# Cross attention of a fused Perceiver block: decay scans in another order, key transposes in 32-column pieces

## The reference, cut to what matters

```python
# first stage: 32 heads of 8, context of 2 x 2048 rows
q = (layernorm(x) @ Wq.T)            # b n (h d)
kv = concat([ctx @ Wk.T, ctx @ Wv.T], -1).reshape(b, m, 32, 8, 2)
k, v = kv[..., 0], kv[..., 1]
q, k = rmsnorm(q), rmsnorm(k)        # over the 8 of a head
x = x + softmax(q k^T / sqrt(8)) v   # over all 2048 context rows
...
# summary of the second block, over the same context
s_t = sigmoid(decay) * s_(t-1) + (ctx_t @ W_in.T + b_in)
summary = mean over t of (s_t @ W_out.T + b_out)
```

## Time and profile before

| | us |
|---|---|
| median of 3 runs | 450.17 |
| lowest, highest | 449.66, 450.70 |
| the profiled execution | 449.79 |
| its span, first to last instruction | 448.0 |
| busy in it: PE, DVE, ACT, POOL | 399.9, 310.7, 250.4, 221.3 |

### The profile page before, as it was taken

The page is one execution under the profiler, slowest core; times in us unless marked ns, Lnnn a source line. Parts: engine busy times, 40 slices in busy tenths (PEclk is TensorE's granted clock), DMA queues, the critical chain, the costliest instruction groups (busy, mean ns, idle before and its releaser), DMA issues.

```text
span 448.0 us, 12553 instructions
## 1 busy us (share of the span) xinstructions
PE 399.9 (89%) x5149; PEld 333.5 (74%) x5149; DVE 310.7 (69%) x697; ACT 250.4 (56%) x494; POOL 221.3 (49%) x269
## 2 busy tenths in 40 slices
PE   6769999999999999879979977789789888999997
PEld 4546666677667777678979955668679877889996
DVE  5677878887888786557798876574998967322221
ACT  2447878778887888775545514521923044544541
POOL 2267656666666773334544620510489742544440
PEclk9979999999999999999999989999899999999999
DMA  4076651543311101620000080250000052000000
GB/s 149 0 262 229 206 172 45 164 127 91 105 32 44 30 15 47 247 113 1 0 1 2 1 321 3 79 244 1 0 2 1 1 227 102 1 0 2 0 2 23
DMA packets 10537, 34.67 MB, mean 77 GB/s; under 512 B 2160, under 2 KB 7280, under 8 KB 8688
## 3 DMA queue, kind: packets, MB, share of 16 engines
q1 hardware_dynamic: 10336, 33.34, 21.4%
q10 hardware_dynamic: 144, 0.52, 0.5%
HBM read 33.60 MB, written 0.26 MB: 76 GB/s over the span
## 4 chain that ended last, share of the span: by engine, by line
PE 52%; DVE 27%; POOL 10%; ACT 5%; issue 4%; DMA 1%; SPq 0%; DVEq 0%; POOLq 0%; ACTq 0%
PE ps L1075 7%; PE ps L1576 7%; PE ps L1532 6%; PE ps L1061 6%; PE ps L1546 3%; PE ps L395 3%; DVE sb_big L1315 2%; PE ps L1563 2%; POOL sb_arena L984 2%; PE ps L456 2%; PE ps L381 2%; DVE sb_arena L1325 2%; PE ps L746 2%; POOL sb_mid L998 2%; DVE sb_big L1313 2%
## 5 line engine op out<-in xcount | busy, mean ns | idle before, releaser
L1499 ACT ACTIVATE sb_arena<-ps 128x1024 f32<-128x1024 f32 x128 | 123.4, 1020 | 26.4 <-PE ps L1563 26.3
L1576 PE MATMUL ps<-sb_arena 128*25 128x128 f32 (+1 forms) x2048 | 69.4, 276 | 0.3 <-ACT sb_arena L1499 0.3
L1576 PEld LDWEIGHTS ps<-sb_arena 128*25 128x25 f32 (+1 forms) x2048 | 50.7, 98 | 7.7 <-ACT sb_arena L1499 0.8
L1532 PE MATMUL ps<-sb_halves 128*128 128x512 f32 x192 | 55.4, 425 | 0.9 <-DVE sb_arena L1325 0.9
L1105 POOL TENSOR_TENSOR sb_halves<-sb_big,sb_halves 128x704 fp32r<-128x704 f32 x20 | 33.7, 1687 | 38.8 <-ACT sb_halves L1099 38.8
L485 POOL TENSOR_TENSOR sb_halves<-sb_big,sb_halves 128x256 fp32r<-128x256 f32 x32 | 23.7, 760 | 44.9 <-ACT sb_halves L469 44.9
L1171 DVE SCALAR_TENSOR_TENSOR sb_arena<-ps,sb_w_q,sb_arena 128x176 f32<-128x176 f32 x40 | 15.9, 401 | 42.7 <-ACT sb_arena L1123 42.5
L1532 PEld LDWEIGHTS ps<-sb_halves 128*128 128x128 f32 x192 | 35.3, 197 | 13.5 <-issue 5.9
L1398 POOL TENSOR_TENSOR sb_big<-sb_arena 128x256 f32<-128x256 f32 x31 | 19.0, 613 | 52.3 <-DVE sb_arena L1286 52.3
L1075 PE MATMUL ps<-sb_halves 128*128 128x352 f32 x240 | 42.9, 332 | 2.0 <-POOL sb_halves L1105 2.0
L1075 PEld LDWEIGHTS ps<-sb_halves 128*128 128x128 f32 x240 | 39.1, 189 | 3.3 <-DVE sb_arena L1171 1.7
(11 more groups left out here) (223 smaller groups left out, 871.0 us busy)
## 6 DMA issues: line engine op xcount, KB each, us to landing
sb_big<-in_w_gu SPq DMA_DIRECT2D x2, 3520.0 KB, 11.8
sb_arena<-in_ctx SPq DMA_DIRECT2D x32, 128.0 KB, 2.3
sb_mid<-in_w_down SPq DMA_DIRECT2D x1, 3584.0 KB, 12.7
sb_mid<-in_w_ffn SPq DMA_DIRECT2D x3, 768.0 KB, 5.3
sb_big<-in_w_q SPq DMA_DIRECT2D x2, 1024.0 KB, 6.5
sb_big<-in_w_k SPq DMA_DIRECT2D x2, 1024.0 KB, 7.1
sb_big<-in_w_v SPq DMA_DIRECT2D x2, 1024.0 KB, 6.0
sb_mid<-in_w_o SPq DMA_DIRECT2D x2, 1024.0 KB, 6.0
```

The costliest lines, as they stand in the source:

```text
L1499: nc.scalar.activation(probs[:, n % P_SLOTS].rearrange("p a g n -> p a (g n)"), ps[:, bank:bank + 2], ACT.Exp, scale=XD ** -0.5).then_inc( ...
L1532: i = T.matmul(ps[:, 7], ctx_half[:, t % 2, c, kt], wkv_half[:, d, kt], start=(n + kt == 0), stop=(n == 2 and kt == KT - 1))
L1576: i = T.matmul(ps[32 * gg:32 * gg + m, 6, j * P:(j + 1) * P], v_sb[:, t % V_SLOTS, 4 * gg + j, head], probs[:, n % P_SLOTS, a, gg], start= ...
```

## The change

- `w_xq` is loaded through ScalarE's DMA queue, behind `w_xkv`, no longer through SyncE's; the load of ScalarE's function table stands ahead of both.
- On VectorE, `decay_rate()` goes to the front of the key work, `decay_weights(0)` behind `mean_squares_q(0)`, `decay_weights(1)` behind `mean_squares(1)`; in the loop, the scan of step t goes from the head of the step to behind `take_v(t + 2)`.
- The value copies of tile 0 go from VectorE to ScalarE, behind the squares of the first keys; `take_queries(1)` goes behind `key_rstd(0)`. The clearing of `v_sb` gets a semaphore of its own.
- On TensorE, `project(1)` goes ahead of `turn_queries(0)`, and four `keep_warm` calls (6, 4, 6 and 4 matmuls) are put into the start.
- In `turn_keys`, each transpose of 128 columns of packed keys becomes four of 32 columns, each into 32 partitions of the output.

```diff
--- before.py
+++ after.py
@@ -201,7 +201,6 @@
             sp.dma_start(x[:], io["x"].rearrange("b l d -> l b d")).then_inc(sem("x_loaded"), 16)
             sp.dma_start(id32[:], io["id32"]).then_inc(sem("x_loaded"), 16)
             sp.dma_start(ctxT[:, 0], io["ctx"][0]).then_inc(sem("ctx_loaded0"), 16)
-            sp.dma_start(w_xq, io["w_xq"]).then_inc(sem("wq_loaded"), 16)
             sp.dma_start(decay[:], io["decay"]).then_inc(sem("decay_loaded"), 16)
             sp.dma_start(ctxT[:, 1], io["ctx"][1]).then_inc(sem("ctx_loaded1"), 16)
             sp.dma_start(id16[:], io["id16"]).then_inc(sem("id16_loaded"), 16)
@@ -1232,7 +1231,8 @@
             V.memset(ones[:], 1.0).then_inc(sem("ones_set"), 1)
             V.memset(zer, 0.0).then_inc(sem("zeros_set"), 1)
             V.memset(xnT[:, :, :, 0:3], 0.0)
-            step(dve, V.memset(v_sb, 0.0))
+            V.memset(v_sb, 0.0).then_inc(sem("v_cleared"), 1)
+            dve.wait_ge(sem("v_cleared"), 1)
             V.memset(v_sb[:, :, :, 8:9], 1.0)
             V.memset(v_sb[:, :, :, 33:34], 1.0)
             dve.wait_ge(sem("x_loaded"), 32)
@@ -1334,27 +1334,26 @@
 
             dve.wait_ge(sem("wkv_high"), 1)
             V.tensor_tensor(wkv_half[:, 1], w_xkv, wkv_half[:, 0].bitcast(F32), ALU.subtract).then_inc(sem("wkv_split"), 1)
+            decay_rate()
             mean_squares_q(0)
+            decay_weights(0)
             take_k(0)
             norm_q(0)
             mean_squares(0)
             pack_q(0)
-            take_v(0)
             pack_keys(0)
             take_k(1)
             take_keys(0)
             take_v(1)
             mean_squares(1)
+            decay_weights(1)
             pack_keys(1)
-            decay_rate()
-            decay_weights(0)
-            decay_weights(1)
             for t in range(NB):
-                if t + 2 < MB:
-                    decay_weights(t + 2)
                 if t + 2 < NB:
                     take_k(t + 2)
                     take_v(t + 2)
+                    if t + 2 < MB:
+                        decay_weights(t + 2)
                     mean_squares(t + 2)
                 if t == 6:
                     take_q(1)
@@ -1456,8 +1455,9 @@
         @block.scalar
         def _(act):
 
+            nc.scalar.preload_act_table_set("natural_log_exp_and_others")
             act.dma_start(w_xkv, io["w_xkv"]).then_inc(sem("wkv_loaded"), 16)
-            nc.scalar.preload_act_table_set("natural_log_exp_and_others")
+            act.dma_start(w_xq, io["w_xq"]).then_inc(sem("wq_loaded"), 16)
             ln_rstd(act, LN_OF["xattn"])
 
             act.wait_ge(sem("wkv_loaded"), 16)
@@ -1482,7 +1482,11 @@
             q_rstd(0)
             act.wait_ge(sem("k_taken"), 1)
             nc.scalar.activation(ksq[:, 0], kraw[:, 0], ACT.Square).then_inc(sem("k_squared"), 1)
-            take_queries(1)
+            act.wait_ge(sem("v_cleared"), 1)
+            for r in range(2):
+                i = nc.scalar.copy(v_sb[:, 0, :, 25 * r:25 * r + 8],
+                                   ps[:, 7, 256 + 128 * r:384 + 128 * r].rearrange("p (h d) -> p h d", d=XD))
+            i.then_inc(sem("kv_taken"), 1)
 
             def key_rstd(t):
                 act.wait_ge(sem("k_meansq"), t + 1)
@@ -1500,6 +1504,7 @@
                                      ACT.Exp, scale=XD ** -0.5).then_inc(sem("exp_done"), 1)
 
             key_rstd(0)
+            take_queries(1)
             act.wait_ge(sem("q_transposed"), 1)
             nc.scalar.copy(qT_x[:, 0], ps[:, 4].bitcast(F16).rearrange("p (g n) -> p g n", g=GROUPS)
                            ).then_inc(sem("q_ready"), 1)
@@ -1543,7 +1548,8 @@
                     pe.wait_ge(sem("q_ready"), 2)
                 out = ps[:, 7 if t else 5].bitcast(F16)
                 for g in range(GROUPS):
-                    i = T.transpose(out[:, g * P:(g + 1) * P], kpack[:, t % 2, g * P:(g + 1) * P], id16[:])
+                    for r in range(0, P, 32):
+                        i = T.transpose(out[r:r + 32, g * P:(g + 1) * P], kpack[:, t % 2, g * P + r:g * P + r + 32], id16[:])
                 i.then_inc(sem("k_transposed"), 1)
 
             def turn_queries(b, bank):
@@ -1592,6 +1598,7 @@
             keep_warm(WARM[LN_OF["xattn"]], 0)
             pe.wait_ge(sem("x_loaded"), 32)
             ln_transpose(pe, LN_OF["xattn"], 0)
+            keep_warm(6, 6)
             pe.wait_ge(sem("xnT_ready"), 1)
             pe.wait_ge(sem("wq_loaded"), 16)
             for b in range(B):
@@ -1601,11 +1608,14 @@
                 if b == 0:
                     project(0)
             pe.wait_ge(sem("zeros_set"), 1)
+            keep_warm(4, 6)
             open_acc()
+            project(1)
+            keep_warm(6, 0)
             pe.wait_ge(sem("id16_loaded"), 16)
             pe.wait_ge(sem("q_packed"), 1)
             turn_queries(0, 4)
-            project(1)
+            keep_warm(4, 0)
             turn_keys(0)
             pe.wait_ge(sem("q_ready"), 1)
             pe.wait_ge(sem("q_copied"), 2)
```

## The result

The changed kernel takes 444.87 us (median of 4 runs, 443.23 to 445.17) against 450.3 us for the kernel before: ratio 0.9873, 95% interval 0.9846 to 0.99. Run again beside other kernels it took 445.17 us, ratio 0.9872 (0.9844 to 0.9901). The profiled execution took 445.03 us with a span of 443.2, 4.8 less than before. The forecast was 441.4 (441.0 for the profiled execution): the direction is right, the time lies in the range, and of the 8.8 us forecast about 5 came.

A forecast was written before the change was run, and what follows sets the result against it. VectorE was taken to bound the start and scan tiles, partly with a low TensorE clock, and TensorE most others. -4.25 - 1.4 - 1.75 - 0.35 - 1.05 = -8.8 us gave 441.0 profiled, 441.4 median; range 438.0 to 447.5.

The forecast's parts named there:

- Start, -4.25: Start of the cross attention: keys 2 copied at 29.8 instead of 34.05 us, 4.25 us gained.
- I expect the clock to stay at 2.4 GHz: Start: with TensorE's gap down to 0.65 us its clock stays high, some 2.6 us of the start's gain.
- rival C: Start: TensorE still falls to 1.2 GHz after another gap, 2.6 us comes back, 444.0 us; chance 0.10.
- D: Loads at the start: x comes earlier and the clock rises earlier, 439 us or a little less; chance 0.06.
- 34 to 71.5 us, -1.4: Seven tiles before 71.5 us: 2 x 0.12, 3 x 0.32 and 0.2 gained, 1.4 us in all.
- The step of the second queries' two tiles (-0.2): Two longer tiles with the second queries' work, 12.7 us for both: 0.2 us gained.
- 71.5 to 97 us, -1.75: Five tiles with the scan moved behind take_v: period 5.07 to 4.75, taken as 0.35 us gained each.
- B: Moved scan collides with GpSimd's work and grows to 1.06 us, 2.7 us of gain goes, 444.1 us; chance 0.09.
- 97 to 111 us and from 132 on, -0.35 and -1.05: Tiles that TensorE bounds, 3 and then 9: key transposes in pieces save 0.12 us a tile.
- Reduction tiles, 0: Four tiles with a reduction of the decay weights: bound by VectorE, so the transposes in pieces change nothing, 0 us.
- Rival A: Key transposes: the pieces don't overlap as the values do, slower, 452.9 us, or about 484 one after another; chance 0.11.
- All later stages follow TensorE, so I let it through whole: Stages after the cross attention: the whole 8.8 us gained there reaches the kernel's end.

The follow-up runs named there:

- no_warm: The changed kernel without its four keep_warm calls; 446.52 us, 0.9932 of the kernel before.
- scan_only: The kernel before with only the loop's scan moved behind take_v; 448.15 us, 0.9939 of the kernel before.
- full_turn: The changed kernel with the key transposes at full width again; 445.56 us, 0.9913 of the kernel before.
- nudge: The changed kernel with one tiny GpSimd memset ahead of the product that weighs the context; 445.57 us, 0.9889 of the kernel before.
- pieces_nudge: The kernel before with only the key transposes in pieces, plus a tiny GpSimd memset ahead of its context product; 452.69 us, 1.0059 of the kernel before.
- pieces_only: The kernel before with the key transposes in 32-column pieces and nothing else; 453.87 us, 1.0063 of the kernel before.
- full_reduce: The changed kernel with full-width transposes and the four decay-weight reductions moved behind take_v; 445.11 us, 0.9894 of the kernel before.
- start_only: The changed kernel with full-width transposes and the loop's scan back at the step's head; 448.2 us, 0.9932 of the kernel before.
- attn_warm: The changed kernel with 12 idle matmuls in TensorE's self-attention gap; 445.47 us, 0.9881 of the kernel before.

## Why the prediction was right and where not

**Start, -4.25: measured -3.85.** The order of events was right: decay rate and scan 0 hidden (12.19), keys 1 turned at 23.64 (forecast 23.95). TensorE's gap fell to 1.36, not 0.65, as TensorE came to it sooner. The step "I expect the clock to stay at 2.4 GHz" failed. This was rival C, mis-sized: it was priced at the whole 2.6 us, but the low stretch was half as long as before and cost 0.8 by no_warm. What made up for half of that was the step before it: scores(0) came at 19.16, not 20.05, mostly because project(0) took 2.30 and not the 2.83 of before (take_k(0) at 13.17 instead of 13.87). x came 0.10 us earlier (5.67 and 5.77), so D's condition hardly held.

**34 to 71.5 us, -1.4: measured -0.7.** The three tiles with a scan gave 0.83, TensorE's two 0.23, as taken. The step of the second queries' two tiles (-0.2) failed, at +0.36. One is GpSimd's: with the scan behind `take_v`, GpSimd's packing product (1.41 instead of 1.30) and the squares behind it come later, and the period is 6.41 instead of 6.12; scan_only, with full transposes, has 6.31. In the other one a run of value products has a stall of TensorE's instructions in it (51.9 us, 1.53 instead of 1.07 for 32): 6.64, where scan_only has 6.28.

**71.5 to 97 us, -1.75: measured -1.43.** Period 4.82, not 4.75. The wait of 0.33 went, as said, but the scan grew by 0.18 where I had left it at 0.48. So B was right in kind; it had the scan grow by 0.58. The idea that L1315's 0.91 might vanish was half right: it did, and L1306 took over the same loss (0.41 to 0.91). In scan_only and full_turn, where it starts later behind GpSimd's product, it takes 0.68.

**97 to 111 us and from 132 on, -0.35 and -1.05: measured -0.32 and -0.96.** The pieces do what they were said to do. The change of shape cost 0.12 us and went.

A group of four f16 pieces starts 0.056 us after the one before it; 0.057 was taken. The Trainium skill (TensorEngine Tiling (Array Packing), Feature Incompatibilities) has column tiling exclude Fast Weight Load; the estimate of 107 ns a group that the prediction worked out with it did not come true: the trace gives half of that, loads included. Whether Fast Weight Load is off, no run shows.

**Reduction tiles, 0: measured +0.49.** I wrote that these four were VectorE's and put the shape of TensorE's work at nothing there. It did matter, by some 20 ns that hand the port to GpSimd; nudge and pieces_nudge show that the order sets the period. I had both orders' lengths in the earlier trace rows (0.43 and 0.91) and didn't ask what sets the order.

**Rival A.** The pieces alone are slower (1.0063), but not as A had it: they overlap fully; what they cost is the port's order and the supply of 1536 more instructions. Neither was in the forecast. In company most of the stalls are gone: the profile after has 0.46 us in the loop (1.53 for 1.07) and 0.34 in the last tile. There too the boundaries come only 2.4 us after the last packet (median), but between 33 and 60 us the packets start at most 3.0 us after the boundary before them, in pieces_only up to 4.4. The stall at matmul 4255 stands in full_turn, full_reduce and start_only too (number 3487, 768 matmuls fewer; that is just six packets), so the pieces are not its cause. In before and scan_only the last boundary of this stage was also passed only 1.45 and 1.40 us after its packet, with no stall inside a run of like matmuls. What makes this packet come so shortly before its boundary in all of them stays open.

**"All later stages follow TensorE, so I let it through whole": failed, 2.0 us.** 0.5 in the last tile, of which 0.34 is this stall:

```profile
174.91 0.84 PE L1582 MATMUL ps<-sb_arena 128*9 128x128 f32 x24
176.09 0.42 PE L1582 MATMUL ps<-sb_arena 128*25 128x128 f32 x8 [0.34 <-issue]
```

1.5 went to the clock in the self attention: with idle matmuls in the gap (attn_warm) the low clock and the loss are gone from the profile, though not from the medians. Together with the 2.0 of the steps above these are the 4.0 us by which the profiled execution is above 441.0.

## What to carry to other kernels

When an engine's instruction becomes shorter or longer by hundredths of a microsecond, look at which pairs of VectorE and GpSimd instructions start within that distance: their order, not their work, may set the period. Count the instructions of an edit as well as their time, since alone the same edit can lose what it gains in company. Here the boundary between two blocks of instructions came some 1.5 us closer to the end of its packet with the pieces, and 21 of 24 stalls are in kernels that have them. And a lead won early is only worth what the later stages let through: in these profiles a low clock behind one gap of the self attention took back 1.4 to 2.8 us from nine versions that came there earlier. The effect of a small edit should therefore be read in its own stage, by the same event in both traces, before the total is believed.

## What the runs showed of the hardware

- Four column pieces of f16 transposes, 32 columns wide, start 6 to 8 ns apart, and the next four 55 to 56 ns after them, loads included (in all but two of the loop's tiles); values and transposes in the same shape next to each other take 0.12 us less than in two.
- VectorE's 32-bit product and GpSimd's product, started 0.01 to 0.02 us apart: 0.41 and 0.99, or 0.98 and 0.72 us, by who is first.
- TensorE's instruction stream comes in packets of 16 KB, 256 instructions each. 24 times in fourteen profiles TensorE stopped at a boundary between two blocks, idle for 0.2 to 1.6 us, and each time it went on 1.25 to 1.61 us after the end of a packet.
- A table load on ScalarE (0.73 to 2.01 us) doesn't hold the DMA issues behind it: w_xkv was issued at 0.76.
- A low granted clock stood behind the same gap of 2.70 us in nine profiles and not in three; in these three the gap came latest.
